# Closing a mixture of experts: token pairs added on VectorE, and bias products 512 columns wide in eight PSUM banks

## The reference

```python
def _L0_ffn_ref(x, gate_w, W1, b1, W2, b2, sW1, sb1, sW2, sb2):   # E = 8, TOP_K = 2, H = 256, F = 1024
    probs = softmax(x_flat @ gate_w.T)
    top_w, sel = top_k(probs, TOP_K);  top_w = top_w / sum(top_w)
    combine = sum(one_hot(sel, E) * top_w[..., None], axis=1)
    h = gelu(einsum('th,ehf->tef', x_flat, W1) + b1)
    y = einsum('tef,efh->teh', h, W2) + b2
    out = einsum('teh,te->th', y, combine)
    return out + gelu(x_flat @ sW1 + sb1) @ sW2 + sb2
x = x + _L0_ffn_ref(...)
```

## Time and profile before

| | us |
|---|---|
| median of 3 runs | 3990.54 |
| lowest and highest run | 3978.85, 4004.24 |
| the profiled execution's own time | 4000.95 |
| its span, first to last instruction | 3999.2 |
| TensorE busy | 3365.5 |
| VectorE busy | 2071.5 |
| ScalarE busy | 1513.3 |
| GpSimd busy | 621.6 |
| mean granted TensorE clock | 0.78 of full |

### The profile page before, as it was taken

The page is one execution under the profiler, slowest core; times in us unless marked ns, Lnnn a source line. Parts: engine busy times, 40 slices in busy tenths (PEclk is TensorE's granted clock), DMA queues, the critical chain, the costliest instruction groups (busy, mean ns, idle before and its releaser), DMA issues. The chain is left out here.

```text
span 3999.2 us, 110373 instructions
## 1 busy us (share of the span) xinstructions
PE 3365.5 (84%) x44512; PEld 2190.4 (55%) x44512; DVE 2071.5 (52%) x8264; ACT 1513.3 (38%) x4247; POOL 621.6 (16%) x361
## 2 busy tenths in 40 slices
PE   7896764899999955669987688899999899999899
PEld 3322441222232314668763344478888888888566
DVE  6314453555555415743326544447777677777454
ACT  3465541555455512656632211232222222222222
POOL 0000000567566731411100000000000000000000
PEclk8678886999999976889977899965555555555999
DMA  1000003000000015011120000100000000000000
GB/s 65 1 1 11 1 1 105 1 1 1 1 1 1 1 49 183 31 38 36 38 85 0 24 0 0 53 3 4 4 4 4 5 4 4 4 4 4 6 7 9
DMA packets 53362, 79.48 MB, mean 20 GB/s; under 512 B 11862, under 2 KB 43307, under 8 KB 51980
## 3 DMA queue, kind: packets, MB, share of 16 engines
q1 hardware_dynamic: 49058, 61.77, 4.6%
q0 software_dynamic: 3408, 9.34, 0.7%
q10 hardware_dynamic: 418, 1.58, 0.1%
HBM read 56.01 MB, written 16.67 MB: 18 GB/s over the span
## 5 line engine op out<-in xcount | busy, mean ns | idle before, releaser
L1303 DVE TENSOR_REDUCE diff_mx<-diff_m_ps 128x1 f32<-128x512 f32 x512 | 329.7, 686 | 353.6 <-PE diff_m_ps L1158 353.6
L2639 PE MATMUL gru_sums<-gru_take,gru_u 128*128 128x4 f16 x12288 | 399.4, 166 | 5.0 <-issue 4.5
L2639 PE MATMUL gru_sums<-gru_keep,gru_u 128*128 128x4 f16 x12288 | 399.4, 166 | 0.0
L2639 PEld LDWEIGHTS gru_sums<-gru_keep,gru_u 128*128 128x128 f16 x12288 | 370.6, 104 | 0.7
L2639 PEld LDWEIGHTS gru_sums<-gru_take,gru_u 128*128 128x128 f16 x12288 | 367.6, 104 | 5.1 <-issue 4.6
L1260 ACT ACTIVATE diff_probs<-diff_s_ps 128x512 f32<-128x512 f32 x512 | 277.9, 595 | 221.6 <-PE diff_s_ps L1152 221.5
L2639 PE MATMUL gru_sums<-gru_rh,gru_u 128*128 128x4 f16 x6144 | 278.3, 169 | 81.5 <-DVE gru_rh L2704 33.4
L1152 PE MATMUL diff_s_ps<-diff_qk 32*128 32x512 f32 x1024 | 292.5, 645 | 63.2 <-DVE diff_mx L1303 55.7
L2639 PEld LDWEIGHTS gru_sums<-gru_rh,gru_u 128*128 128x128 f16 x6144 | 235.9, 106 | 123.9 <-DVE gru_rh L2704 123.9
L1158 PE MATMUL diff_m_ps<-diff_qk 32*128 32x512 f32 x1024 | 294.2, 651 | 6.4 <-DVE diff_mx L1303 6.4
L1349 POOL TENSOR_TENSOR diff_sums<-diff_sums,diff_probs 128x2048 f32<-128x2048 f32 x64 | 289.4, 4522 | 31.4 <-ACT diff_probs L1260 31.1
(11 more groups left out here) (471 smaller groups left out, 5800.0 us busy)
## 6 DMA issues: line engine op xcount, KB each, us to landing
moe_weights<-in_L_ffn_W SPq DMA_DIRECT2D x16, 1024.0 KB, 12.8
expert_slots<-diff_blank SPq DMA_DIRECT2D x1, 5031.0 KB
stream_a<-expert_slots SPq DMA_DIRECT2D x39, 129.0 KB, 2.0
lora_w<-in_L_cond_w_R SPq DMA_DIRECT2D x1, 4096.0 KB
moe_both<-expert_pairs SPq DMA_DIRECT2D x4, 1024.0 KB, 9.6
stream_b<-in_x SPq DMA_DIRECT2D x4, 512.0 KB, 10.5
hyp_wf<-in_L_cond_w_f SPq DMA_DIRECT2D x2, 1024.0 KB, 8.4
stream_b<-in_xT SPq DMA_DIRECT2D x1, 2048.0 KB, 13.5
```

The lines of the kernel that those rows point to most:

```text
L1303: dve.tensor_reduce(mx[:, i % 2, kt, at:at + 1], m_ps[:, m % 3, :], X_AXIS, ALU.max).then_inc(ph.maxes_ready, 1)
L2639: last = pe.matmul(sums[:, par, g, m * B:(m + 1) * B], part[:, g, c, m * P:(m + 1) * P], state[:, c * B:(c + 1) * B], start=False, stop=(l ...
```

## The change

The two bias loads move from SP to ScalarE's queue. VectorE adds the two rows of all tokens of a group in place, one addition of 128x1024 for each group, signalled by `made`. `sums` takes all eight PSUM banks, one for each unit, and the transposed weights use the upper four of them before the bias products do. TensorE makes all eight bias products first, 512 columns wide, one for each bank; then for each unit it waits for the group's addition and makes four identity products instead of eight. The wait for a free bank is gone.

```diff
-        turn_ps = inner.enter_context(nc.psum_tensor("moe_turn_ps", [P, 4, T], F32))
-        sum_ps = inner.enter_context(nc.psum_tensor("moe_sum_ps", [P, 4, T], F32))
+        sums = inner.enter_context(nc.psum_tensor("moe_sum_ps", [P, DC * B, T], F32))
...
             @block.sync
             def _(sp):
-                sp.dma_start(b2[0:E, :], io["L0_ffn_b2"]).then_inc(ph.bias_loaded, 16)
-                sp.dma_start(b2[E:E + 1, :], io["L0_ffn_sb2"].unsqueeze(0)).then_inc(ph.bias_loaded, 16)
...
+            @block.scalar
+            def _(act):
+                act.dma_start(b2[0:E, :], io["L0_ffn_b2"]).then_inc(ph.bias_loaded, 16)
+                act.dma_start(b2[E:E + 1, :], io["L0_ffn_sb2"].unsqueeze(0)).then_inc(ph.bias_loaded, 16)
+
             @block.tensor
             def _(pe):
                 for t in range(NT):
-                    last = pe.transpose(turn_ps[0:E + 1, t // TT, t % TT * P:(t % TT + 1) * P], comb[:, t, :], ident[:, :])
+                    last = pe.transpose(sums[0:E + 1, B + t // TT, t % TT * P:(t % TT + 1) * P], comb[:, t, :], ident[:, :])
                 last.then_inc(ph.turned, 1)
+                pe.wait_ge(ph.bias_loaded, 32)
                 pe.wait_ge(ph.rows_copied, 1)
-                pe.wait_ge(ph.bias_loaded, 32)
-                for g in range(B):
-                    pe.wait_ge(ph.tile_loaded[g], 16)
-                    for c in range(DC):
-                        u = DC * g + c
-                        if u >= 4:
-                            pe.wait_ge(ph.out_taken, u - 3)
-                        for t in range(TT):
-                            cols = sum_ps[:, u % 4, t * P:(t + 1) * P]
-                            pe.matmul(cols, b2[:, c * P:(c + 1) * P], combT[:, (TT * g + t) * P:(TT * g + t + 1) * P],
-                                      start=True, stop=False)
-                            for k in range(CHOICES):
-                                last = pe.matmul(cols, both[:, g, t, k, c * P:(c + 1) * P], ident[:, :], start=False,
-                                                 stop=(k == CHOICES - 1))
-                        last.then_inc(ph.out_ready, 1)
+                for u in range(DC * B):
+                    g, c = divmod(u, DC)
+                    pe.matmul(sums[:, u, :], b2[:, c * P:(c + 1) * P], combT[:, g * T:(g + 1) * T], start=True, stop=True)
+                for u in range(DC * B):
+                    g, c = divmod(u, DC)
+                    pe.wait_ge(ph.made, g + 1)
+                    for t in range(TT):
+                        last = pe.matmul(sums[:, u, t * P:(t + 1) * P], both[:, g, t, 0, c * P:(c + 1) * P], ident[:, :],
+                                         start=False, stop=True, skip_group_check=True)
+                    last.then_inc(ph.out_ready, 1)
 
             @block.vector
             def _(dve):
                 dve.wait_ge(ph.turned, 1)
...
+                def add_pairs(g):
+                    dve.wait_ge(ph.tile_loaded[g], 16)
+                    dve.tensor_tensor(both[:, g, :, 0, :], both[:, g, :, 0, :], both[:, g, :, 1, :], ALU.add).then_inc(ph.made, 1)
+
+                add_pairs(0)
+                for g in range(B):
+                    if g + 1 < B:
+                        add_pairs(g + 1)
+                    for c in range(DC):
+                        dve.wait_ge(ph.out_ready, DC * g + c + 1)
+                        dve.tensor_tensor(x2T[:, c, g * T:(g + 1) * T], sums[:, DC * g + c, :], x1T[:, c, g * T:(g + 1) * T], ALU.add)
```

More of the change, by code:

```diff
@@ L2064, in _ @@
                 dve.wait_ge(ph.turned, 1)
[L2065 to L2070, removed]
+                dve.tensor_copy(combT[:, :], sums[0:E + 1, B:2 * B, :].rearrange("e a n -> e (a n)")).then_inc(ph.rows_copied, 1)
+                def add_pairs(g):
[8 more added lines that the diff above has]
+                        dve.tensor_tensor(x2T[:, c, g * T:(g + 1) * T], sums[:, DC * g + c, :], x1T[:, c, g * T:(g + 1) * T], ALU.add)
         in_flight.rejoin()
```

## The result

The changed kernel takes 3961.49 us, the median of 8 runs (3951.66 to 3972.45), beside 4001.89 us of 8 runs of the kernel before. The measured ratio, which is not the quotient of the two medians, is 0.9917, 95% interval 0.9893 to 0.9940: 0.8% faster, 24 to 43 us, and not clearly past 1%. The medians alone lie 40.4 us, 1.0%, apart. The profiled span went from 3999.2 to 3954.6 us, but 9 of these 44.6 us lie ahead of the stage that was changed: it begins at 2049.78 us instead of 2058.8. So the stage is measured by itself from here on, from its first transposition to the start of its last VectorE sum: 66.5 us before, 29.2 us after. That is 37.2 us; from the last sum to the end both kernels take nearly the same, 1873.9 and 1875.5 us.

What follows compares the result with a forecast made beforehand. The closing of the experts was taken as bound by TensorE issuing small f32 products. 0.5 us earlier start plus 60.0 us of products less 24.05 us gave 36.4 us, taking the median 3990.54 to 3954.1 us; range 3940 to 3974.

Steps and rivals of the forecast that it cites:

- Pace: Closing of the experts: uninterrupted identity records take 0.213 us each at the lower clock, 0.11 us at the upper.
- rival 1: Identity products keep the old mixture's mean pace, 0.312 us a record: 20.0 us, gain 26.7 us, time 3963.8 us; 12%.
- the 4-row stretch: From 27 to 45 us, gapless 4-row, 512-column products stayed at clock 0.50; 9-row bias products were taken to do likewise.
- Rival 2: Clock rises already in the bias products; identity products start at 2073.7, gain 43.0 us, time 3947.5 us; 10%.
- the layout: Forecast timeline of the closing's TensorE groups and VectorE work: identity products from 2078.4, last sum at 2088.9, 36.4 us gained.
- A2: VectorE's addition for group 2, 1.23 us, queued behind the sums of group 0; forecast done at 2084.15.
- A3: VectorE's addition for group 3, 1.23 us, queued behind the sums of group 1; forecast done at 2086.8.
- Rival 4: Bias rows arrive late on ScalarE's queue, delaying the first product 0 to 9.6 us; gain 27 to 36 us; 10%.
- Rivals 5 and 6: Slower, as the linear stage loses clock, 3%; TensorE and VectorE take turns in the closing, gain 22 us, 2%.

Runs made afterwards that it cites:

- Before_pad128: The kernel before with its bias operands filled with zeros to 128 partitions; stage 30.0 us against 66.5, whole-kernel ratio to before 0.9931.
- bias_on_sp: The changed kernel with the two bias loads back on SP, ahead of the tiles; stage 30.7 us, one run.
- after_pad64: The changed kernel with bias operands filled with zeros to 64 partitions; stage 29.7 us, one run.
- after_pad128: The changed kernel with bias operands filled with zeros to 128 partitions; stage 23.0 us, whole-kernel ratio to before 0.9908.
- warm_start: after_pad128 with all four additions ahead of the sums and 32 extra transpositions in the first attention stage; whole-kernel ratio to before 0.9814.

## Why the prediction was right

**Pace.** Taken from four records of one group, 0.213 us at the lower and 0.11 us at the upper clock. Measured: 26 records in 5.5 us and 37 in 4.5 us. The choice against the mean of 0.312 us (rival 1) was the step that mattered most: with the mean, 20.0 us were put down for what took 10.55. Before_pad128 shows that its reason holds too, the change between operands of few and many rows.

**The bias products.** 13.65 us were predicted and 12.6 measured, 0.85 us each; the 1 us is three records at the upper clock, which the transpositions had raised, a thing the prediction left out. This microsecond is luck of the profiled execution: in bias_on_sp the clock didn't rise and the stretch took 13.9 us. That they keep the clock low came from the 4-row stretch, and after_pad64 and after_pad128 confirm the reason. Rival 2 came true only where the operands were filled to 128 rows. The Trainium skill (TensorE: Matmul & The Clock Gate, section "Why this matters for your kernels") says that TensorE gets past the lower clock by being kept busy without a gap; dense products of 4, 9 and 64 rows here did not.

**The clock in the identity products.** Predicted 4 us after they begin, measured 5.8 (2068.43 to about 2074.2). That term was too small: some 8 records more ran at the lower pace, 0.10 us each, 0.9 us. The sum hardly shows it, as another term was too large: in the layout TensorE waits 0.15 us for A2 and 0.8 us for A3, and since it came later in fact, it waited for A3 alone, 0.3 us. So the 64 records took 10.55 us, pause included, where the layout had 10.4. That the two nearly cancel was not foreseen.

**VectorE.** Additions of 1.20 to 1.23 us, predicted 1.23. The wait for A3 was predicted under 1 us and is 0.3. The layout's last sum at 30.1 us after the stage's start (2088.9 less 2058.8) was 29.2 in fact.

**What is moved.** Nothing, as predicted: 6.03 us to the first product with either queue. Rival 4 is excluded for this place. A small load beside 1 MB tiles on another queue was not late, if with little to spare.

**The sum.** 36.4 us predicted, 37.2 measured in the stage, 1 us of it luck. For the whole kernel 0.91% was predicted, and 0.83% with an interval of 0.60 to 1.07% measured, 3961.49 us beside 3954. The predicted time is 7.5 us low because it was counted from 3990.54 us, the median of three runs, and the kernel before has 4001.89 over 8, 11.4 us more; the rest, 4 us the other way, is within the noise. The runs' scatter, which the prediction took as given, comes for the larger part from one stage: in the eleven profiles without extra transpositions the first attention stage takes 160 us five times, 175 and 190 us three times each, by the moment when its clock rises. What is left of the twelve spans without this stage and the closing agrees within 13 us. Rivals 5 and 6 didn't occur.

**What the halving earned.** The prediction didn't divide the gain. Order alone gives 30.5 us, the additions on top of it 6.8, the additions alone 12.6. And full rows alone give 36.5 us, nearly the whole change, with a fill of 2 us on a VectorE that is idle then.

## What to carry to other kernels

Before products are counted, look at their pace and at the granted clock beside the number of rows that they use: a dense stream of products with 9 or 64 rows of 128 stayed at half clock, and each switch between such a product and a full one cost some 0.3 us at that clock. Filling the short operand with zeros up to 128 rows gets both back. Gathering all short products ahead of the full ones gets the switches back, and the clock only once the short ones are done. Where a long stage sits at the lower clock in some executions, a few microseconds of full-row transpositions inside it may be worth tens; here they were worth 6 to 36 us, in the one profile taken.

## What the runs showed of the hardware

- The slow steps: 0.35 and 0.37 us, onto and after the first f32 record of 128 columns when 9-row or 64-row and 128-row operands take turns, 0.213 us where rows are equal, at the lower clock. It was not measured at the upper clock.
- In dense streams of one kind of product the number of rows decided whether the clock rose, not columns or values: 18 us with 4 rows, 10.9 us with 9 rows and 9 us with 64 rows, all of 512 columns, stayed at 0.50; the same products with 119 rows of zeros rose to 1.00 within 5 us. This is no rule for every mixture: in the first attention stage, where score products of 16 rows alternate with full ones, the clock did rise, late, and then held.
- Transpositions can raise the clock: sixteen of them, 3.57 us, had it at 1.00 from 2053.8 in the kernel after and in six other profiles, though not in the remaining five, and with 32 in warm_start it was up from 158 us to the end of the stage. The Trainium skill (TensorE: Matmul & The Clock Gate, section "Part 4: PE-mode transpose") says that the full clock doesn't engage for transpositions, as they don't count as busy in the same way; for these f32 ones the measurement decides, and it did engage.
- Whether the slow steps arise in the weight loads or in the array stays open, and so does what number of rows between 64 and 128 would do; no run here tells.
